# Another instruction order in a fused attention and feed-forward kernel: the last element, the early squares, the folded weights, row 3's routing, maximum 0

## The chip, the cores and the metric

One core of a Trainium2 chip runs the whole kernel. The metric is the device time of one execution in microseconds (us). Three runs of the kernel before gave 920.5 us as their median (919.33 to 921.06).

## The reference, cut to what matters

For each of 16 batch elements (`x` and `ctx` are 128 x 1024, all in float32):

```
def attention(q, k, v, Wq, Wk, Wv, Wo, bo, g):         # q = layernorm(x), k = v = ctx
    qh = softmax(Wq q over each head's 64 rows) / 8     # 8 heads of 64
    kh = softmax(Wk k over the 1024 columns)
    out = Wo (context(kh, Wv v) applied to qh) + bo
    return out / max(norm(out over the 128 rows), 1e-12) * g * sqrt(128)

x = x + tanh(g_xattn) * attention(...)
# feed-forward on y = layernorm(x): 64 experts of rank 16, the top 16 by score
scores = y Wr^T;  gates = softmax(top 16 scores)
h = y A^T (64 x 16 values per row), each expert's 16 times its gate
x = x + tanh(g_ffn) * (h B) * 2
```

## The kernel before, in words

Every product in float32 is made of three passes of 512, 448, 384 or 256 columns on TensorE (helper `three_pass`, lines 59 to 63): a rounded high part and a low part (the remainder) of each operand. ScalarE copies the high part out of PSUM (names `hi_...`) and VectorE subtracts it to give the low part (names `lo_...`).

**Attention stage.** The function `body(b, head, tail, ahead)` is written once for each engine. Body b does the head of element b (queries, keys, their maxima and exponentials, transposes) and the tail of element b-1 (context product, the fold of `Wv` and `Wo` into it, output), and loads the next element. It is laid out for b = 0 and 1, looped for the middle, and laid out for b = 14 (`NB - 2`), 15 (`NB - 1`, called `last` on VectorE) and 16 (tail alone). Each engine runs its instructions in the order in which they are written here; semaphores alone tie the engines together. There is no planner: the order is written by hand.

Steps that matter below, with their lines in the profile:

- queries of block p of 128 columns: TensorE `mm_q` into `psQ`; VectorE `max_q` (L1013); TensorE `shift_q` (L1491) adds the negated maximum; ScalarE `exp_q` (L678, and L685 for block 3); POOL `halve` (L447) and VectorE `sum_q` (L1018, L1021) give the sum; POOL `normalise` (L454); TensorE `tr_q` (L1510) transposes; ScalarE `hi_q` (L693), VectorE `lo_q` (L1027).
- keys of block j: TensorE `mm_k` into `psK`; VectorE `max_k` (L1007); ScalarE `exp_k` (L670); TensorE `tr_k` (L1501); ScalarE `hi_k` (L700), VectorE `lo_k` (L1038).
- context: TensorE `context` (24 passes); ScalarE `hi_kc` (L711), VectorE `lo_kc` (L1043), TensorE `fold` (12 passes of 256 columns), VectorE `scale_m` (L1055), ScalarE `hi_m` (L715), POOL the low part (L546), TensorE `output`, ScalarE `out_o` (L728). Elements 0 to 2 also square their output (L727) and VectorE sums the squares (`part_early`, L969); TensorE's `sum_early` and VectorE's `early_guess` start an inverse square root from them, which POOL finishes.
- in body 0, TensorE multiplies `Wv` and `Wo`; ScalarE (L867) and VectorE (L1304) split the product.
- in body 15, elements 0 and 1 are carried towards the feed-forward part: ScalarE `scale_first` (L742), VectorE `spread` (L1003), POOL `spread_first` and `add_first`, VectorE `stats2_sums` (L1071, L1073) and `std2`, ScalarE `normalise` (L763).

**Feed-forward stage.** Row b of `ffn_body` does for element b: TensorE `up` in three pieces, `sum_u` (L1566) for the norm of element b+2, `down` for element b-1. VectorE routes (`route_step` 0 to 10: copy of scores, top 8, negated maximum, second top 8, gates), multiplies by the gates (L1145), transposes (L1161, L1178). ScalarE exponentiates the scores (`exp_scores`, L811, after step 2), normalises element b+1's input, moves 32 x 256 groups (`move_y`, `move_h`, L778), makes high parts, squares `u` (`square_u`, L750). Row 3 (`third`) runs seven steps of the norm of element 5 before it waits for `h`.

What ScalarE has in row b stands in this order, and the order isn't changed:

```
hi_moved_h(b - 1)
normalise(b + 1, (j + 2) % SLOTS)
exp_scores(b)
move_y(b + 1, j % 2)
hi_moved_y(b + 1)
move_h(b)
square_u(b + 3, ...)
```

## Time and profile before

| | before |
|---|---|
| median of 3 runs | 920.5 us (919.33 to 921.06) |
| the profiled execution, its own time | 921.38 us |
| its span in the trace | 919.5 us |
| mean granted TensorE clock | 0.996 of full |
| TensorE matmul busy | 898.3 us (98%) |
| VectorE busy | 737.2 us (80%) |
| ScalarE busy | 680.6 us (74%) |
| POOL busy | 520.1 us (57%) |

A line of a timeline gives the start in us from the beginning of the span, the duration in us, the engine, the line, the operation, what it writes and reads, and how many instructions of the kind are merged; in brackets at the end stand the time for which the engine was idle before it and what ended that. PE is TensorE, DVE is VectorE, ACT is ScalarE. An operation's duration overlaps the next one's by some 0.07 to 0.1 us on DVE and ACT, and a matmul's (0.39 us for 512 columns) far more, so the distance from start to start is what an instruction costs its engine.

### The profile page before, as it was taken

The numbers are of one execution on the slowest core, as the hardware profiler recorded it, in microseconds if no ns is written. First come the engines' busy times: TensorE is split into PE (matmuls) and PEld (weight loads), VectorE is DVE, ScalarE is ACT, GpSimd is POOL, SyncE is SP. The second block draws the span as 40 slices with busy tenths as digits, with TensorE's granted clock in tenths as the row PEclk, the third lists the DMA queues.
The fourth block names the chain that finished last, engine by engine and source line by source line (L and its number), as shares of the span: only waits on it lengthen the run. The fifth ranks groups of instructions, "written<-read, shape, count | busy, mean of one in ns | idle before, by whom it ended". The sixth has DMA issues, their size and how long they took to land.

```text
span 919.5 us, 15914 instructions
## 1 busy us (share of the span) xinstructions
PE 898.3 (98%) x4732; PEld 760.7 (83%) x4732; DVE 737.2 (80%) x1531; ACT 680.6 (74%) x1392; POOL 520.1 (57%) x342
## 2 busy tenths in 40 slices
PE   7899999999999999999999999999999999999998
PEld 5687887878888888888887799988899989999996
DVE  6888899888888888888887878897877768777642
ACT  4787787687678768777877748678888878888731
POOL 3686777788798789879778958231222212222100
PEclk9999999999999999999999999999999999999999
DMA  4323524443453544344232694112222111212001
GB/s 160 115 82 129 178 78 156 163 144 111 161 185 108 168 139 127 109 135 156 91 115 69 207 354 165 67 68 69 76 71 70 67 64 69 70 67 69 24 24 46
DMA packets 35325, 104.09 MB, mean 113 GB/s; under 512 B 4432, under 2 KB 11600, under 8 KB 35280
## 3 DMA queue, kind: packets, MB, share of 16 engines
q1 hardware_dynamic: 29520, 82.59, 26.2%
q0 software_dynamic: 5472, 20.45, 7.5%
q10 hardware_dynamic: 288, 0.52, 0.1%
q8 instruction: 19, 0.31, 0.1%
q14 instruction: 26, 0.21, 0.1%
HBM read 79.43 MB, written 24.12 MB: 113 GB/s over the span
## 4 chain that ended last, share of the span: by engine, by line
PE 63%; DVE 16%; issue 7%; ACT 7%; POOL 5%; DMA 1%; ACTq 0%; DVEq 0%; POOLq 0%
PE ps L61 19%; PE ps L63 18%; PE ps L62 18%; PE ps L1501 4%; PE ps L1510 3%; DVE qmax L1013 2%; ACT h_raw L778 2%; DVE kmax L1007 2%; PE ps L1491 2%; DVE qT_lo L1027 1%; DVE mt L1055 1%; ACT y_raw L778 1%; ACT qT_hi L693 1%; POOL x L528 1%; POOL qe L454 1%
## 5 line engine op out<-in xcount | busy, mean ns | idle before, releaser
L525 POOL TENSOR_TENSOR rb<-u_in,rb 128x1024 f32<-128x1024 f32 x14 | 33.7, 2410 | 219.0 <-DVE rb L1003 219.0
L454 POOL TENSOR_TENSOR qe<-qe,qrec 128x1024 f32<-128x1024 f32 x64 | 121.2, 1903 | 28.9 <-DVE qrec L1021 28.9
L61 PE MATMUL ps<-aT_hi,yT_hi 128*128 128x448 f32 (+2 forms) x360 | 119.9, 333 | 1.8 <-DVE hg L1145 1.3
L62 PE MATMUL ps<-aT_hi,yT_lo 128*128 128x448 f32 (+2 forms) x360 | 118.7, 330 | 0.0
L63 PE MATMUL ps<-aT_lo,yT_hi 128*128 128x448 f32 (+2 forms) x360 | 118.6, 330 | 0.0
L1027 DVE TENSOR_TENSOR qT_lo<-ps,qT_hi 128x512 fp32r<-128x512 f32 x128 | 82.1, 683 | 42.6 <-ACT qT_hi L693 42.6
L778 ACT ACTIVATE h_raw<-hg 32x256 f32<-32x256 f32 x248 | 103.0, 415 | 17.0 <-DVE hg L1178 14.2
L447 POOL TENSOR_TENSOR qhalf<-qe 128x512 f32<-128x512 f32 x64 | 82.3, 1286 | 32.7 <-ACT qe L685 30.8
L778 ACT ACTIVATE y_raw<-u_in 32x256 f32<-32x256 f32 x216 | 89.5, 414 | 5.8 <-DVE u_in L1161 3.5
L61 PE MATMUL ps<-bT_hi,hT_hi 128*128 128x512 f32 x240 | 93.7, 390 | 0.0
L62 PE MATMUL ps<-bT_hi,hT_lo 128*128 128x512 f32 x240 | 93.5, 390 | 0.0
L63 PE MATMUL ps<-bT_lo,hT_hi 128*128 128x512 f32 x240 | 93.4, 389 | 0.0
L678 ACT ACTIVATE qe<-ps 128x1024 f32<-128x1024 f32 x48 | 49.2, 1025 | 46.4 <-PE ps L1491 46.4
L693 ACT ACTIVATE qT_hi<-ps 128x512 fp32r<-128x512 f32 x128 | 70.7, 598 | 14.9 <-PE ps L1510 13.6
L1007 DVE TENSOR_REDUCE kmax<-ps 128x1 f32<-128x1024 f32 x64 | 77.9, 1216 | 4.0 <-PE ps L63 2.4
L670 ACT ACTIVATE ek<-ps,kmax 128x1024 f32<-128x1024 f32 x64 | 72.3, 1130 | 4.7 <-DVE kmax L1007 3.0
L61 PEld LDWEIGHTS ps<-aT_hi,yT_hi 128*128 128x128 f32 x360 | 68.5, 190 | 5.0 <-issue 1.7
L1510 PE MATMUL ps<-ident,qe 128*128 128x128 f32 x512 | 69.1, 275 | 1.7 <-DVE ekT_lo L1038 1.5
L62 PEld LDWEIGHTS ps<-aT_hi,yT_lo 128*128 128x128 f32 x360 | 68.4, 190 | 2.1
L63 PEld LDWEIGHTS ps<-aT_lo,yT_hi 128*128 128x128 f32 x360 | 68.5, 190 | 1.8
L1510 PEld LDWEIGHTS ps<-ident,qe 128*128 128x128 f32 x512 | 58.0, 140 | 14.0 <-DVE ekT_lo L1038 3.3
L700 ACT ACTIVATE ekT_hi<-ps 128x512 fp32r<-128x512 f32 x100 | 54.5, 601 | 16.0 <-PE ps L1501 16.0
(180 smaller groups left out, 2556.3 us busy)
## 6 DMA issues: line engine op xcount, KB each, us to landing
x_in<-in_x SPq DMA_DIRECT2D x16, 512.0 KB, 4.2
ctx_in<-in_ctx SPq DMA_DIRECT2D x16, 512.0 KB, 4.7
ctxT_in<-in_ctxT SPq DMA_DIRECT2D x16, 512.0 KB, 3.3
ctxT_hi<-in_ctxT POOLq DMA_DIRECT2D x16, 512.0 KB, 3.7
u_scratch<-osb SPq DMA_DIRECT2D x16, 512.0 KB, 2.9
x<-in_x SPq DMA_DIRECT2D x15, 512.0 KB, 4.0
out<-res SPq DMA_DIRECT2D x15, 512.0 KB, 2.9
turn_scratch<-ek SPq DMA_DIRECT2D x14, 512.0 KB, 5.7
```

The lines of the kernel that those rows point to most:

```text
L61: nc.tensor.matmul(psum, whi, mhi, start=start, stop=False)
L62: nc.tensor.matmul(psum, wlo, mhi, start=False, stop=False)
L63: return nc.tensor.matmul(psum, whi, mlo, start=False, stop=stop)
L447: nc.gpsimd.tensor_tensor(qhalf[:, p % 2, :].rearrange("p (h d) -> p h d", d=DH // 2), v[:, :, 0:DH // 2], v[:, :, DH // 2:DH], ALU.add).t ...
L454: nc.gpsimd.tensor_tensor(v, v, w, ALU.mult).then_inc(q_norm, 1)
L670: nc.scalar.activation(to, of, ACT.Exp, bias=kmax[:, j:j + 1], accum_out=ksum[:, j:j + 1]).then_inc(k_exp, 1)
L693: nc.scalar.activation(qT[0][:, :, n * P:n * P + P], psT[:, h, :].rearrange("p (j n) -> p j n", n=P), ACT.Copy).then_inc(q_hi, 1)
L700: nc.scalar.activation(ekT[0][:, 4 * h:4 * h + 4, j * P:j * P + P], psT[:, h, :].rearrange("p (n d) -> p n d", d=P), ACT.Copy).then_inc(k_ ...
L778: last = nc.scalar.activation(dst[32 * q:32 * q + 32, 256 * a:256 * a + 256], src[32 * a:32 * a + 32, 256 * q:256 * q + 256], ACT.Copy)
L1007: nc.vector.tensor_reduce(kmax[:, j:j + 1], psK, axis=AX.XY, op=ALU.max, negate=True).then_inc(k_max, 1)
L1027: nc.vector.tensor_tensor(qT[1][:, :, v], psT[:, h, :].rearrange("p (j n) -> p j n", n=P), qT[0][:, :, v].bitcast(f32), ALU.subtract).then ...
L1510: last = nc.tensor.transpose(psT[:, h, j * P:j * P + P], qe[:, p, w:w + P], ident[:, :])
```

## The change

It moves instructions inside the hand-written order of ScalarE, VectorE and TensorE; none is added, removed or resized, and no semaphore wait is added. On ScalarE: in body 15, the two scalings of elements 0 and 1 come later and the normalisation of element 0 goes from the end of body 15 to behind the last exponentials of queries in body 16; in body 0, the high part of the folded weights comes after three other steps. On VectorE: maximum 0 of the queries precedes the context's low part in every body but the first; the sum of early squares comes some nine steps earlier in bodies 2 to 4; in body 0 the low part of the folded weights comes later; in body 14 the guess for the early norms comes later; in body 15 both spreads come later, and the low part of key block 2 precedes the statistics of element 0 and the sum of query block 1; in row 3 three steps of routing come first and the norm's steps stand together. On TensorE: in body 16 a transpose of queries precedes that of element 0's rows, in body 14 the sum of the early squares follows the context.

```diff
--- before.py
+++ after.py
@@ -813,12 +813,14 @@
             def body(b, head, tail, ahead, early=False):
                 if tail:
                     exp_q(b - 1, 3)
+                if tail and not head:
+                    normalise(0, 0)
                 if head:
                     hi_xn(b, 1)
+                if tail:
+                    hi_kc(b - 1)
                 if head and not ahead:
                     scale_first(0)
-                if tail:
-                    hi_kc(b - 1)
                 if tail and not head:
                     hi_y(0)
                     hi_q(b - 1, 1)
@@ -858,23 +860,23 @@
                     norm_x(b + 1)
                     hi_ctx(b + 1, 0)
                     hi_ctx(b + 1, 1)
+                if head:
+                    hi_k(b, 1)
+                    exp_k(b, 3)
+                if tail:
+                    hi_q(b - 1, 3)
                 if head and not ahead:
                     scale_first(1)
-                if head:
+                if tail and head:
+                    out_o(b - 1, 0, early)
+                if head:
+                    exp_q(b, 2)
                     if not started(b):
                         act.wait_ge(fold_done, 1)
                         for par in range(2):
                             nc.scalar.activation(wvo[0][:, :, par * P:par * P + P],
                                                  psX[:, par, :].rearrange("p (j o) -> p j o", o=P),
                                                  ACT.Copy, scale=DH ** -0.5).then_inc(fold_hi, 1)
-                    hi_k(b, 1)
-                    exp_k(b, 3)
-                if tail:
-                    hi_q(b - 1, 3)
-                    if head:
-                        out_o(b - 1, 0, early)
-                if head:
-                    exp_q(b, 2)
                 if ahead:
                     hi_xn(b + 1, 0)
                 if head:
@@ -889,8 +891,6 @@
                     out_o(b - 1, 1, early)
                 if head:
                     hi_q(b, 0)
-                if head and not ahead:
-                    normalise(0, 0)
 
             exp_k(0, 0)
             body(0, head=True, tail=False, ahead=True)
@@ -1042,6 +1042,16 @@
                 dve.wait_ge(kc_hi, b + 1)
                 nc.vector.tensor_tensor(kc[1][:, :], psX[:, 0, :], kc[0][:, :].bitcast(f32),
                                         ALU.subtract).then_inc(kc_lo, 1)
+
+            def low_fold():
+
+                dve.wait_ge(fold_hi, 2)
+                for par in range(2):
+                    nc.vector.scalar_tensor_tensor(wvo[1][:, :, par * P:par * P + P],
+                                                   psX[:, par, :].rearrange("p (j o) -> p j o", o=P),
+                                                   DH ** -0.5,
+                                                   wvo[0][:, :, par * P:par * P + P].bitcast(f32),
+                                                   ALU.mult, ALU.subtract).then_inc(fold_lo, 1)
 
             def scale_m(b):
 
@@ -1250,24 +1260,24 @@
                     turn_k(b)
                 if ahead and started(b):
                     stats(b + 1)
-                if norms:
-                    early_guess()
                 if ahead and started(b):
                     std(b + 1, range(3))
                 if tail and ahead:
                     sum_q(b - 1, 3)
+                if head and started(b):
+                    max_q(b, 0)
+                if norms:
+                    early_guess()
                 if tail:
                     lo_kc(b - 1)
                 if tail and not head:
                     sum_q(b - 1, 3)
                 if head and started(b):
-                    max_q(b, 0)
                     max_k(b, 1)
+                if early:
+                    part_early(b - 2)
                 if last:
                     sum_q(b - 1, 3)
-                if last:
-                    dve.wait_ge(ctx_lo, 2 * NB)
-                    spread(0, rb_first[0], n_newton, 4 * NEWTON)
                 if tail and not head:
                     lo_y(0)
                     lo_q(b - 1, 1)
@@ -1275,6 +1285,9 @@
                     lo_q(b - 1, 1)
                 if tail:
                     scale_m(b - 1)
+                if last:
+                    dve.wait_ge(ctx_lo, 2 * NB)
+                    spread(0, rb_first[0], n_newton, 4 * NEWTON)
                 if tail and not head:
                     stats2(1, 1)
                     lo_q(b - 1, 2)
@@ -1299,18 +1312,6 @@
                         dve.wait_ge(tanh_done, 1)
                         nc.vector.tensor_scalar(gcol[:, :], g_raw[:, 2:3], gates[:, 0:1], math.sqrt(C),
                                                 ALU.mult, ALU.mult).then_inc(gcol_done, 1)
-                        dve.wait_ge(fold_hi, 2)
-                        for par in range(2):
-                            nc.vector.scalar_tensor_tensor(wvo[1][:, :, par * P:par * P + P],
-                                                           psX[:, par, :].rearrange("p (j o) -> p j o", o=P),
-                                                           DH ** -0.5,
-                                                           wvo[0][:, :, par * P:par * P + P].bitcast(f32),
-                                                           ALU.mult, ALU.subtract).then_inc(fold_lo, 1)
-                if last:
-                    dve.wait_ge(xn_lo, 2 * NB)
-                    spread(1, rb_first[1], n_newton, 4 * NEWTON)
-                if early:
-                    part_early(b - 2)
                 if tail and not head:
                     route(0)
                 if tail:
@@ -1321,13 +1322,20 @@
                 if head:
                     dve.wait_ge(k_exp, 4 * b + 4)
                     nc.vector.reciprocal(krec[:, :], ksum[:, :]).then_inc(k_rec, 1)
+                if last:
+                    dve.wait_ge(xn_lo, 2 * NB)
+                    spread(1, rb_first[1], n_newton, 4 * NEWTON)
                 if ahead:
                     max_k(b + 1, 0)
+                if head and not last:
+                    sum_q(b, 1)
+                if head:
+                    lo_k(b, 2)
+                if not started(b):
+                    low_fold()
                 if last:
                     stats2_sums(0, 0)
-                if head:
                     sum_q(b, 1)
-                    lo_k(b, 2)
                 if last:
                     std2(0, range(4))
                 if head:
@@ -1386,11 +1394,13 @@
                     lo_moved_y(3)
                     spread_u(4)
                 elif third:
-                    norm_steps(5, range(7))
+                    for n in range(3):
+                        route_step(3, n)
                     lo_moved_h(2)
                     turn_y(4, 0)
-                    norm_steps(5, range(7, NRT))
-                    route(3)
+                    norm_steps(5, range(NRT))
+                    for n in range(3, TOP):
+                        route_step(3, n)
                     spread_u(5)
                 else:
                     result(b - 2, (j + 1) % 2, (j + 3) % SLOTS, 2 * i + (j - 1) // 2)
@@ -1627,8 +1637,8 @@
                 if not head:
                     context(b - 1, 0)
                     context(b - 1, 1)
+                    tr_q(b - 1, 1, next(turn))
                     tr_y(0, 0)
-                    tr_q(b - 1, 1, next(turn))
                     fold(b - 1)
                     up(0, 0)
                     tr_q(b - 1, 2, next(turn))
@@ -1640,11 +1650,11 @@
                     up(0, 2)
                     return
 
-                if isinstance(b, int) and b == NB - 2:
-                    sum_early()
                 if tail:
                     context(b - 1, 0)
                     context(b - 1, 1)
+                if isinstance(b, int) and b == NB - 2:
+                    sum_early()
                 if head:
                     if not started(b):
                         pe.wait_ge(wq_low, 1)
```

## Rows read from the trace of the kernel before

**Rows 1.** The page's first part: busy time, share of the span, instructions.

```profile
PE 898.3 (98%) x4732; PEld 760.7 (83%) x4732; DVE 737.2 (80%) x1531; ACT 680.6 (74%) x1392; POOL 520.1 (57%) x342
```

**Rows 2.** Timeline, DVE and then PE, of body 12, one of the loop.

```profile
399.76 0.65 DVE L1043 TENSOR_TENSOR kc_lo<-ps,kc_hi 128x512 fp32r<-128x512 f32 x1
400.45 1.22 DVE L1013 TENSOR_REDUCE qmax<-ps 128x16 fp32r<-128x1024 f32 x1
...
404.06 1.29 DVE L1027 TENSOR_TENSOR qT_lo<-ps,qT_hi 128x512 fp32r<-128x512 f32 x2 [1.03 <-ACT qT_hi L693]
...
401.72 0.70 PE L1491 MATMUL ps<-qmax,ident_r 128*128 128x512 f32 x2
...
403.05 0.36 PE L61 MATMUL ps<-wvo_hi,kc_hi 128*128 128x256 f32 x1
```

**Rows 3.** Timeline, DVE and then PE, of body 3, whose tail is an early element.

```profile
110.67 0.63 DVE L1043 TENSOR_TENSOR kc_lo<-ps,kc_hi 128x512 fp32r<-128x512 f32 x1
111.22 1.21 DVE L1013 TENSOR_REDUCE qmax<-ps 128x16 fp32r<-128x1024 f32 x1
...
114.82 1.29 DVE L1027 TENSOR_TENSOR qT_lo<-ps,qT_hi 128x512 fp32r<-128x512 f32 x2 [1.27 <-ACT qT_hi L693]
...
127.13 1.23 DVE L969 TRANSPOSE_TENSOR_REDUCE part<-osq 128x1024 f32 x1
...
112.48 0.48 PE L1491 MATMUL ps<-qmax,ident_r 128*128 128x512 f32 x1 [0.33 <-DVE qmax L1013]
```

**Rows 4.** Timeline, ACT and then DVE, of body 0.

```profile
27.15 1.06 ACT L867 ACTIVATE wvo_hi<-ps 128x512 fp32r<-128x512 f32 x2
...
30.06 1.28 DVE L1304 SCALAR_TENSOR_TENSOR wvo_lo<-ps,wvo_hi 128x512 fp32r<-128x512 f32 x2
...
36.16 1.21 DVE L1013 TENSOR_REDUCE qtop<-ps 128x16 f32<-128x1024 f32 x1
```

**Rows 5.** Timeline, DVE, ACT and then PE, of body 15, the last with a head.

```profile
499.87 1.19 DVE L1003 STREAM_TRANSPOSE rb_first<-nr 128x1024 f32<-128x1024 f32 x1
...
516.58 1.25 DVE L1071 BATCH_NORM_STATS2 bn<-x 128x6 f32<-128x512 f32 x2
...
518.94 1.22 DVE L1038 TENSOR_TENSOR ekT_lo<-ps,ekT_hi 128x512 fp32r<-128x512 f32 x2
...
521.84 1.28 DVE L1038 TENSOR_TENSOR ekT_lo<-ps,ekT_hi 128x512 fp32r<-128x512 f32 x2
...
511.30 1.15 ACT L742 ACTIVATE u_first<-u_first,gcol 128x1024 f32<-128x1024 f32 x1 [1.48 <-DMA u_first<-u_scratch]
...
517.25 1.09 ACT L700 ACTIVATE ekT_hi<-ps 128x512 fp32r<-128x512 f32 x2
...
505.61 0.50 PE L61 MATMUL ps<-qT_hi,mt_hi 128*128 128x512 f32 x1 [1.21 <-POOL mt_lo L546]
...
522.66 1.16 PE L1510 MATMUL ps<-ident,qe 128*128 128x128 f32 x8 [0.38 <-DVE ekT_lo L1038]
```

**Rows 6.** Timeline of the feed-forward rows 2 to 5: DVE, ACT and then PE.

```profile
611.96 1.24 DVE L1161 STREAM_TRANSPOSE u_in<-u_in 128x1024 f32<-128x1024 f32 x1
...
614.68 0.35 ACT L811 ACTIVATE ex<-sc,neg_top 128x64 f32<-128x64 f32 x1 [2.83 <-DVE neg_top L1104]
614.94 6.81 ACT L778 ACTIVATE y_raw<-u_in 32x256 f32<-32x256 f32 x16
...
600.76 0.44 PE L61 MATMUL ps<-aT_hi,yT_hi 128*128 128x448 f32 x1 [1.33 <-DVE hg L1145]
...
624.54 0.47 PE L61 MATMUL ps<-aT_hi,yT_hi 128*128 128x448 f32 x1 [0.41 <-DVE yT_lo L1173]
...
654.85 0.40 PE L1566 MATMUL ps<-part,sel 128*128 128x32 f32 x2 [2.14 <-DVE part L1209]
```

**Rows 7.** Busy time by stretch: after the stretch, its length, PE, PEld, DVE, ACT, POOL busy (instructions), granted clock, DMA share, GB/s.

```profile
31.00:34.00 3.00, 3.00 (x11) 2.45 (x10) 1.42 (x3) 0.87 (x3) 2.83 (x2) 0.50 0.09 29
...
655.00:659.00 4.00, 4.00 (x16) 4.00 (x17) 3.34 (x11) 1.92 (x5) 0.00 (x0) 0.57 0.62 217
```

## The prediction

> **What bounds the kernel now.** I read the page first, then the timeline engine by engine at each moved instruction, then the granted clock of the stretches around TensorE's long waits. TensorE is busy for 98% of the span [rows 1], and its passes follow each other at a fixed distance through nearly all of it. So a moved instruction matters only where TensorE stands still, or where the move makes it stand still. Four places have such stalls near the edits: bodies 2 to 4, where the shift of query block 0 waits for its maximum (0.33 us in body 3) [rows 3]; body 15 (1.21 us for the low part of the scaled context, 0.38 us for a low key part) [rows 5]; the feed-forward rows 2 to 5 (1.33, 0.41 and 2.14 us) [rows 6]; and body 0. Two of them drag a second cost behind them: TensorE worked at a granted clock of 0.50 in 31 to 34 us and 0.57 in 655 to 659 us [rows 7], its 1.2 GHz level for most of that time, which costs 3 x 0.50 = 1.5 us and 4 x 0.43 = 1.7 us.
>
> **Maximum 0 ahead of the context's low part, in the loop.** The maximum starts at 400.45, right behind the low part of 399.76, and looks delayed by it. It isn't: its six passes ended at about 400.41, as the low part did. With the new order VectorE waits for TensorE and starts at the same 400.45. The low part then ends at about 400.45 + 1.15 + 0.65 = 402.25, later by 1.85 us; behind it stand the key maximum (0.45 us later) and the low query part, which has 1.03 us of idle time before it that absorbs this. Who waits for the low part is the fold, at 403.05: 0.8 us of slack is left. The transpose and the shift at 401.72 see no difference [rows 2]. I take 0 for each of the twelve undisturbed bodies. Bounds: gain of 0.03 each (the distance of the two starts), loss of 0.1 each should the slack be smaller than it looks.
>
> **Bodies 2 to 4.** Here VectorE is late. The low part begins at 110.67, the maximum at 111.22, though its input was there at 110.80, so the new order starts it at 110.84: 0.38 us earlier, and 0.55 in body 2. But the sum of early squares, 1.23 us, now stands between key maximum 1 and the low query part at 114.82, in an idle time of 1.27 us [rows 3]. Step by step for body 3: maximum 110.84, context's low part 111.98, key maximum 112.53, sum of squares 113.65, low query part 114.81. That is where it begins today. Behind it stand the scaling by the sums, its high and low parts, and the output, which TensorE waits for. So the stall moves from the shift to the output. I take -0.2 for body 2, 0 for 3 and 4. Bounds: -1.3 (all three gains kept), +0.5 (the sum costs more than the gain). Taking the sum away from its old place at 127.13 gains nothing, since VectorE waits there for ScalarE a few steps on.
>
> **Body 0.** The high part of the folded weights (1.06 us) leaves the path to the exponentials of key block 3, which hold TensorE until 30.33; but the transpose ends only at 27.5, so about 0.6 is gained there, and POOL's second low part of the next context, ending at 31.0, holds the rest. The low part of the folded weights (1.28 us) leaves a place where VectorE was idle anyway and lands right before query maximum 3 at 36.16 [rows 4], on the path to the transpose that starts the context product. Gain of 1.0 upstream against 1.2: +0.2. Bounds: -0.9 (the half clock of 31 to 34 us disappears too) and +0.8.
>
> **Body 14.** Two small VectorE steps and one small matmul change place within slack; the fold waits for the first of them, which is done 1 us before it. 0, bounds -0.2 and +0.3.
>
> **Body 15, first half.** The spread (1.19 us) stood before the low query part and delayed the chain to the output at 505.61. Moved behind the scaling, it frees 1.1 us, of which the order of the maximum takes back 0.35: -0.77 there. The spread now delays query maximum 1 and key maximum 2 by 0.3, so at the transpose of query block 3 about 0.5 is left.
>
> **Body 15, second half.** ScalarE's second scaling (1.15 us at 511.30) moves behind the high part of query block 3, right ahead of the output's copy, exponentials 2 and the high part of key block 2. That one, at 517.25 today, comes at 517.55: 0.5 to 0.8 gained ahead, 1.06 lost. VectorE's low part of key block 2 can start 0.62 later, at 518.17. Behind it now stand the element's statistics and the sum of query block 1, which today run from 516.58 to 518.94 (2.36 us), while VectorE idles before 518.17. Low key part 3, today 2.90 us behind low part 2, starts at 518.17 + 2.36 + 2.90 = 523.43, not 521.84; the transpose of query block 0, 0.82 behind that, at 524.25, not 522.66 [rows 5]. The whole body is 1.6 us longer, and TensorE is idle for 2.9 us in one piece. POOL's normalisation of query block 1 waits for that sum; behind it are queued its DMA issues for the `A` weights and two additions, all about 1.3 us later, with the users later by as much. SP's loads wait for the end of the context and shift with it.
>
> **The clock there.** An idle time of 2.14 us was followed by the low level, one of 1.33 us was not [rows 6, 7]. After 2.9 us I expect a stretch at 1.2 GHz, part of which falls into the idle time: half to all of 1.7 us, I take +1.0. Bounds 0 and 1.9.
>
> **Body 16.** Element 0's normalisation leaves the place ahead of exponentials 3 and comes right behind them; those follow the late transpose, so they end when they do today. Two transposes change places. The rows of element 0 are ready when TensorE gets there: 0, bounds -0.2 and +0.5, since VectorE's low part of them is within 0.2 us of the path.
>
> **Row 3.** ScalarE waits for 2.83 us for the negated maximum, and behind that wait stands the moving of element 4's groups at 614.94, whose input is ready at 613.2 [rows 6]. With the three steps of routing first, the groups move 1.7 us earlier. The norm steps that VectorE did in idle time now come behind: gates and transpose are 0.6 later, so ScalarE's second move starts 1.3 earlier. The stall at 624.54 (0.41) goes; the one at 654.85 ends the same chain (moves, squares, sum of squares), so it ends 1.3 earlier, and since TensorE is 0.4 ahead by then, 1.3 us is the net gain and the stall shrinks from 2.14 to about 1.2. That is below the 1.33 that left the clock alone, so I take the 1.7 us of slow clock back as well, rounded up to 1.8 with the slow restart: -3.1. Bounds: -0.4 and -3.8.
>
> **Sum.** +0.2 - 0.2 + 1.6 + 1.0 - 3.1 = -0.5 us. The profiled execution took 921.4 us, the median of the runs 0.9 less, 920.5; the difference is applied to the median: 920.0 us. About 0.2% (1.8 us) is what a measurement of this kernel can tell from no change.
>
> **A rule on the clock.** The Trainium skill, TensorE: Matmul & The Clock Gate, Part 1, says that half clock is the default state which activity lifts, and that the monitor runs free of the kernel's start, so that its switches fall differently from run to run. The trace agrees that long idle times come before the low level; one trace can't show the scatter. By that rule both clock terms would be even chances, +0.5 and -0.9, and the sum would be +0.3.
>
> **Rivals.**
> - *All four gains hold* (chance 0.28). The early bodies keep their 1.3 us, and TensorE keeps its clock after the gap of body 15. For it: the sum of squares fits into 1.27 us of idle time to within 0.04 [rows 3], and an overlap of 0.1 decides. Against it: the working above uses those overlaps already. 0.2 - 1.3 + 1.6 - 3.1 = -2.6: 917.9 us.
> - *The clock decides against the change* (0.15, slower). The place is body 15's gap before the context. It costs the full 1.7 behind 1.6, and the shorter gap in row 5 still ends in the low level, so only 1.3 is gained there. It decides if the low level can follow a gap as short as 1.2 us; body 0 speaks for it, where it came after a wait shorter than 1.5. 0.2 - 0.2 + 3.3 - 1.3 = +2.0: 922.5.
> - *The loop pays* (0.08, slower). If the fold's slack of 0.8 is gone, for example because the low part waits longer behind the maximum, each of 13 bodies loses 0.2: -0.5 + 2.6 = +2.1: 922.6.
> - *Row 3's stall isn't set by ScalarE's moves* (0.05, slower). Then the reorder doesn't do what it says, POOL's residual sets the time, and only 0.4 is gained: +2.2: 922.7.
> - The forecast holds the remaining 0.44, with a range of its own of 918.6 to 921.6; 0.06 of it lies more than 0.2% below.
>
> So faster by over 0.2%: 0.28 + 0.06 = 0.34; slower: 0.28; within: 0.38. The range of 917.0 to 923.2 takes in the first rival's bound and all the slower ones, each with half a microsecond more.
>
> **What would show it.** Right: the shift of query block 0 in the loop keeps its distance of 1.27 us from the start of its maximum; in body 3 the stall before it goes and the one before the output grows; the output in body 15 starts about 0.8 earlier, but the transpose before the context about 1.6 later, behind low key part 3; ScalarE's wait for the negated maximum in row 3 nearly goes, and the sum in row 5 waits about 1.2 us, with a clock of 1.00 behind it. Wrong: a fold that waits for the context's low part; a gap before the context below 1 us; a clock near 0.5 still standing behind row 5's sum.

## The result, and the profile after

The changed kernel takes 923.35 us (median of 5 runs, 922.31 to 925.61), the kernel before 920.5 us in the runs beside it (919.33 to 921.75). The ratio is 1.0033 with a 95% interval of 1.0018 to 1.0049: slower by 2.9 us, where 0.5 us faster was forecast, and just above the range.

The profiled execution took 922.31 us, 0.9 more than that of before: it was the fastest of its five, while that of before was above its median. So the traces explain 0.9 of the 2.9 us directly. The trace of before holds two stretches at the low clock level and that of after one, so the two aren't equal in this; the part on the clock comes back to it.

The page's first part, of after. Busy times are those of [rows 1] to within 1.8 us, in a span 1.0 us longer: no work was added, so the change is all in waits.

```profile
span 920.5 us, 15914 instructions
PE 897.1 (97%) x4732; PEld 758.9 (82%) x4732; DVE 738.2 (80%) x1531; ACT 680.4 (74%) x1392; POOL 520.5 (57%) x342
```

Both traces are cut at the same TensorE instructions. Each row is the distance of two starts, in us of the profiled executions:

| stretch | before | after | difference | forecast |
|---|---|---|---|---|
| start to the first context pass (body 0) | 39.03 | 39.27 | +0.24 | +0.2 |
| its context pass in body 2 to that in body 5 | 97.96 | 97.39 | -0.57 | -0.2 |
| fold of body 5 to fold of body 13 (loop) | 256.53 | 256.43 | -0.10 | 0 |
| fold of body 13 to fold of body 14 | 32.25 | 33.39 | +1.14 | 0 |
| fold of body 14 to row 0's up part | 65.42 | 68.46 | +3.04 | +2.6 |
| row 0's up part to row 5's sum | 122.11 | 120.87 | -1.24 | -1.3 |
| row 5's sum to row 6's | 24.69 | 23.13 | -1.56 | -1.8 |

They add up to +0.95, the difference of the spans to 0.01, and row 6's sum to the last one is 161.85 us in both. One row is far from the forecast by its path: body 14. This is its timeline, of after, DVE, POOL and then PE.

```profile
464.04 1.23 DVE L1013 TENSOR_REDUCE qmax<-ps 128x16 fp32r<-128x1024 f32 x1 [0.67 <-PE ps L63]
465.18 0.25 DVE L995 TENSOR_SCALAR ns<-ps 128x96 f32<-128x96 f32 x1
465.46 1.90 DVE L67 TENSOR_SCALAR nr<-ns 128x96 int32<-128x96 int32 x1
467.28 0.68 DVE L1043 TENSOR_TENSOR kc_lo<-ps,kc_hi 128x512 fp32r<-128x512 f32 x1
...
463.54 3.76 POOL L454 TENSOR_TENSOR qe<-qe,qrec 128x1024 f32<-128x1024 f32 x2
...
468.02 0.39 PE L61 MATMUL ps<-wvo_hi,kc_hi 128*128 128x256 f32 x1 [1.12 <-DVE kc_lo L1043]
```

The root step of the early norms, line 67 on 128 x 96 numbers, takes 1.90 us. In the trace of before the same instruction, ahead of the context's low part, took 0.21 us:

```profile
462.44 0.20 DVE L995 TENSOR_SCALAR ns<-ps 128x96 f32<-128x96 f32 x1
462.67 0.21 DVE L67 TENSOR_SCALAR nr<-ns 128x96 int32<-128x96 int32 x1
463.99 0.68 DVE L1043 TENSOR_TENSOR kc_lo<-ps,kc_hi 128x512 fp32r<-128x512 f32 x1
...
464.02 3.77 POOL L454 TENSOR_TENSOR qe<-qe,qrec 128x1024 f32<-128x1024 f32 x2
```

In the old place POOL's halving ended 0.14 us after the root began (461.52 + 1.29 = 462.81). In the new order it comes while POOL multiplies the query block by its reciprocal sums (two instructions of 1.9 us). It ends at 465.46 + 1.90 = 467.36, about when the second of these does (463.54 + 3.76 = 467.30). The context's low part stands behind it, and the fold, which has 0.8 us of slack in the loop by the prediction's working, waits: 1.12 us by the row, 1.37 us counted from where its next pass could have started.

The trace of before holds the same sight already, in row 1 of the feed-forward part: a small step of the routing, SBUF to SBUF, takes 1.83 us and ends at 572.21, with POOL's fourth instruction of a row (561.66 + 10.49 = 572.15). In the 15 other feed-forward rows it takes 0.25 or 0.26 us.

```profile
570.38 1.83 DVE L1130 TENSOR_SCALAR gate<-gsel,grec 128x64 f32<-128x64 f32 x1
...
561.66 10.49 POOL L484 TENSOR_TENSOR bT_lo<-b_raw,bT_hi 128x1024 fp32r<-128x1024 f32 x4
```

Body 15, of after, DVE, ACT and then PE:

```profile
516.62 1.21 DVE L1003 STREAM_TRANSPOSE rb_first<-nr 128x1024 f32<-128x1024 f32 x1
518.88 1.29 DVE L1038 TENSOR_TENSOR ekT_lo<-ps,ekT_hi 128x512 fp32r<-128x512 f32 x2 [1.05 <-ACT ekT_hi L700]
520.09 1.28 DVE L1081 BATCH_NORM_STATS2 bn<-x 128x6 f32<-128x512 f32 x2
521.64 0.63 DVE L1018 TENSOR_REDUCE qsum<-qhalf 128x16 f32<-128x512 f32 x1
523.06 1.21 DVE L1013 TENSOR_REDUCE qtop<-ps 128x16 f32<-128x1024 f32 x1
524.19 1.28 DVE L1038 TENSOR_TENSOR ekT_lo<-ps,ekT_hi 128x512 fp32r<-128x512 f32 x2
...
515.73 1.14 ACT L742 ACTIVATE u_first<-u_first,gcol 128x1024 f32<-128x1024 f32 x1
518.25 1.09 ACT L700 ACTIVATE ekT_hi<-ps 128x512 fp32r<-128x512 f32 x2
...
505.47 0.50 PE L61 MATMUL ps<-qT_hi,mt_hi 128*128 128x512 f32 x1 [0.44 <-POOL mt_lo L546]
525.02 1.94 PE L1520 MATMUL ps<-ident,qe 128*128 128x128 f32 x8 [2.65 <-DVE ekT_lo L1038]
```

The output's wait fell from 1.21 to 0.44 us [rows 5], and the transpose of query block 0 waits 2.65 us for the last low key part, with TensorE idle for 2.81 us in one piece (2.9 was forecast). Low key part 2 could start at 518.88, and low key part 3 starts 5.31 us behind it, where it was 2.90 [rows 5].

Body 0, of after: VectorE's low part of the folded weights stands right ahead of query maximum 3, as forecast. What wasn't forecast is in the last row:

```profile
30.54 1.10 ACT L877 ACTIVATE wvo_hi<-ps 128x512 fp32r<-128x512 f32 x2
35.20 1.28 DVE L1050 SCALAR_TENSOR_TENSOR wvo_lo<-ps,wvo_hi 128x512 fp32r<-128x512 f32 x2
36.39 1.22 DVE L1013 TENSOR_REDUCE qtop<-ps 128x16 f32<-128x1024 f32 x1
37.52 1.28 DVE L1038 TENSOR_TENSOR ekT_lo<-ps,ekT_hi 128x512 fp32r<-128x512 f32 x2
...
31.04 0.50 PE L61 MATMUL ps<-ctx_hi,wk_hi 128*128 128x512 f32 x1 [0.20 <-POOL ctx_lo L413]
38.35 1.16 PE L1520 MATMUL ps<-ident,qe 128*128 128x128 f32 x8 [2.36 <-DVE ekT_lo L1038]
```

The wait before the transpose that opens the context product was [1.16] in the trace of before (1.53 us of idle time), and is 2.36 (2.72 us idle). Ahead of it nearly nothing was gained, since the keys of block 1 now wait for POOL's low part (31.04).

The loop and the feed-forward rows went as forecast. Body 12 (maximum, context's low part, shift) and row 5's sum, of after:

```profile
399.98 1.22 DVE L1013 TENSOR_REDUCE qmax<-ps 128x16 fp32r<-128x1024 f32 x1 [0.63 <-PE ps L63]
401.12 0.68 DVE L1043 TENSOR_TENSOR kc_lo<-ps,kc_hi 128x512 fp32r<-128x512 f32 x1
...
401.26 0.70 PE L1501 MATMUL ps<-qmax,ident_r 128*128 128x512 f32 x2
402.59 0.36 PE L61 MATMUL ps<-wvo_hi,kc_hi 128*128 128x256 f32 x1
...
604.53 0.44 PE L61 MATMUL ps<-aT_hi,yT_hi 128*128 128x448 f32 x1 [1.35 <-DVE hg L1155]
627.75 0.36 PE L61 MATMUL ps<-aT_hi,yT_hi 128*128 128x448 f32 x1
657.35 0.40 PE L1576 MATMUL ps<-part,sel 128*128 128x32 f32 x2 [1.51 <-DVE part L1219]
```

The shift follows the start of its maximum by 1.28 us, as by 1.27 before [rows 2]. Row 3's stall of 0.41 is gone, and row 5's has fallen from 2.14 to 1.51 [rows 6]. By stretch, of after (columns as in [rows 7]):

```profile
31.00:34.00 3.00, 2.96 (x17) 2.44 (x17) 1.93 (x3) 2.69 (x6) 3.00 (x2) 1.00 0.05 12
38.00:44.00 6.00, 5.64 (x29) 4.76 (x30) 5.12 (x9) 4.92 (x19) 1.33 (x2) 1.00 0.14 57
525.00:528.00 3.00, 2.98 (x11) 2.75 (x12) 2.75 (x9) 1.60 (x5) 3.00 (x6) 0.50 0.93 267
657.00:660.00 3.00, 2.65 (x16) 2.66 (x17) 2.82 (x5) 1.13 (x1) 0.00 (x0) 1.00 0.96 339
```

The low level stands behind body 15's stall alone; in the trace of before it stood in body 0 and behind row 5's stall.

### The profile page after: what moved, and what is told of

It is laid out like the page before. It is cut to its first block, busy times and chain, and to the rows that moved or that the text cites. A ratio compares the mean times of both kernels' runs of the same rounds, so it can differ in the third digit from the quotient of the medians.

```text
span 920.5 us, 15914 instructions
## 1 busy us (share of the span) xinstructions
PE 897.1 (97%) x4732; PEld 758.9 (82%) x4732; DVE 738.2 (80%) x1531; ACT 680.4 (74%) x1392; POOL 520.5 (57%) x342
## 4 chain that ended last, share of the span: by engine, by line
PE 71%; DVE 16%; ACT 5%; issue 5%; POOL 2%; DMA 0%; DVEq 0%; ACTq 0%; POOLq 0%
PE ps L61 21%; PE ps L63 20%; PE ps L62 20%; PE ps L1520 5%; PE ps L1511 4%; ACT h_raw L778 3%; DVE kmax L1007 2%; DVE qmax L1013 2%; PE ps L1501 1%; DVE mt L1065 1%; DVE qT_lo L1027 1%; POOL x L528 1%; DVE ekT_lo L1038 1%; DVE hg L1188 1%; POOL rb L525 1%
## 5 line engine op out<-in xcount | busy, mean ns | idle before, releaser
L1013 DVE TENSOR_REDUCE qmax<-ps 128x16 fp32r<-128x1024 f32 x48 | 58.6, 1221 | 14.0 <-PE ps L63 13.2
```

Source lines behind the costliest of these rows:

```text
L1013: nc.vector.tensor_reduce(top[:, p % 2, :], psQ.rearrange("p a (h d) -> p (a h) d", d=DH), axis=AX.X, op=ALU.max, negate=True).then_inc(q_ ...
```

## The experiments

In the diffs, lines with + are the experiment's. Times are medians with the lowest and highest run; kernels of one batch share the runs of before. The stretches of all kernels, in us of the profiled executions:

```
                      ctx 1   bodies  loop    fold 13  fold 14  row 3 up  sum 5   idle    idle
                      to 2    2 to 5  5-13    to 14    to up 0  to sum 5  to 6    body 0  body 15
before                31.80   97.96   256.53  32.25    65.42    54.09     24.69   1.53    0.54
after                 31.79   97.39   256.43  33.39    68.46    52.82     23.13   2.72    2.81
body 14 back          33.36   97.39   256.45  32.21    67.19    52.82     23.15   2.73    2.84
root reads PSUM       33.05   97.44   256.50  32.01    67.20    52.82     23.15   2.73    2.82
row 3 alone           31.80   97.90   256.49  32.24    65.30    52.82     23.15   1.53    0.50
body 15 back          33.31   97.37   256.47  33.38    65.92    52.82     23.15   2.73    0.56
statistics back       33.18   97.39   256.44  33.39    65.90    52.85     24.69   2.73    0.56
body 0 back           31.84   97.41   256.41  33.39    68.71    52.83     24.70   1.53    2.80
squares back          33.90   96.50   256.43  33.40    67.14    52.82     24.71   2.73    2.82
first try             31.80   96.56   256.43  32.23    67.24    52.83     24.69   1.53    -
row 3 and maximum 0   31.79   96.54   256.55  32.18    65.58    52.81     23.15   1.53    0.49
with the late spread  31.83   96.50   256.54  32.20    65.24    52.81     23.14   1.53    0.54
three places back     31.82   97.40   256.42  32.20    65.97    52.81     23.15   1.54    0.56
```

"ctx 1 to 2" is from the first context pass to the next, "bodies 2 to 5" from context pass to context pass, "up 0" row 0's up part, "sum 5 to 6" from row 5's sum to row 6's, "idle" TensorE's idle time before the first query transpose of a context product, counted from where its next pass could have started, which is 0.15 to 0.38 us more than the wait in brackets. Two columns show the clock: "ctx 1 to 2" is 31.8 where the granted clock stays at 1.00, and 33.05 to 33.90 where a low stretch lies in it; "sum 5 to 6" is 23.15 or 24.7 in the same way, so that stretch costs 1.55 us.

**Body 14 undone.** VectorE's root step goes back ahead of the context's low part, and TensorE's summing pass ahead of the context passes; all else is the changed kernel.

```
+                if norms:
+                    early_guess()
                 if ahead and started(b):
                     std(b + 1, range(3))
...
-                if norms:
-                    early_guess()
                 if tail:
                     lo_kc(b - 1)
```

> The changed kernel with body 14 as it was before: the guess of the early norms ahead of the context's low part and of query maximum 0, and TensorE's small sum ahead of the context. Theory (the guess's second step, held for 1.90 us behind POOL's normalisation, delays the context's low part and so the fold): the wait of 1.37 us before the fold at 468.0 us goes, the distance between the first fold passes of bodies 14 and 15 drops from 31.7 us of the changed kernel by some 1.4, and the median by 1.3 to 1.6 us, to about 921.9. Rival (body 14 only looks longer, since body 15 takes back what it loses): the wait goes but the fold of body 15 comes no earlier, and the time stays at 923.3.

Measured: 922.20 us (921.32 to 923.43), ratio 1.0016 [1.0008, 1.0025], beside 920.95 for before. The interval overlaps that of the changed kernel, so here and in the next runs the place is shown by the trace, and the median agrees with it. The two folds are 32.21 us apart again, 1.18 less than in the changed kernel, and the root takes 0.21 us:

```profile
463.72 0.21 DVE L67 TENSOR_SCALAR nr<-ns 128x96 int32<-128x96 int32 x1
466.84 0.68 DVE L1043 TENSOR_TENSOR kc_lo<-ps,kc_hi 128x512 fp32r<-128x512 f32 x1
...
468.31 0.36 PE L61 MATMUL ps<-wvo_hi,kc_hi 128*128 128x256 f32 x1
```

So 1.2 us of the loss is made in body 14. Here body 15's stall of 2.84 us had no low level behind it, while a stretch in body 1 did, where the changed kernel's trace has 1.00:

```profile
38.00:41.00 3.00, 2.76 (x13) 2.30 (x14) 2.16 (x5) 2.08 (x8) 1.12 (x1) 0.70 0.29 119
41.00:44.00 3.00, 3.00 (x11) 2.45 (x10) 2.95 (x5) 2.91 (x13) 0.54 (x1) 0.73 0.09 38
525.00:528.00 3.00, 2.60 (x15) 2.23 (x16) 2.82 (x10) 1.94 (x7) 3.00 (x6) 1.00 0.93 271
```

**The root reads PSUM.** Order and wait stay as in the changed kernel; only the source of the root step is the sums in PSUM and not their copy in SBUF. That leaves out the lower bound on the sums for the root.

```
-                first_root(r, s).then_inc(n_guess, 1)
+                first_root(r, psN_early.rearrange("p (e n) -> p e n", e=EARLY)).then_inc(n_guess, 1)
```

> The changed kernel, with the order as it is, but the guess's second step (the first root) reads the sums in PSUM rather than their copy in SBUF; it leaves out the floor under the sum for this first guess, which no value reaches. Theory (the step of 1.90 us has one input and one output in SBUF and waits for the port that POOL's running multiplication holds): with its input in PSUM it takes about 0.2 us as at its old place, the context's low part starts 1.7 us earlier, and the fold waits 0 to 0.2 us. First rival (the step is held by its semaphore or by the queue): it still takes 1.9 us and the fold still waits 1.3. Second rival (the place itself is too late, whatever the step takes): the fold still waits by 1 us or more.

Measured: 922.85 us (921.19 to 923.92), ratio 1.0022 [1.0012, 1.0032], which doesn't tell it from the changed kernel. Timeline of body 14, DVE and POOL, of this kernel:

```profile
467.96 0.25 DVE L995 TENSOR_SCALAR ns<-ps 128x96 f32<-128x96 f32 x1
468.25 0.26 DVE L67 TENSOR_SCALAR nr<-ps 128x96 int32<-128x96 int32 x1
468.42 0.68 DVE L1043 TENSOR_TENSOR kc_lo<-ps,kc_hi 128x512 fp32r<-128x512 f32 x1
...
466.33 3.77 POOL L454 TENSOR_TENSOR qe<-qe,qrec 128x1024 f32<-128x1024 f32 x2
468.20 1.91 POOL L454 TENSOR_TENSOR qe<-qe,qrec 128x1024 f32<-128x1024 f32 x1
```

The last row is the second of the two multiplications by itself. The root starts 0.05 us behind it, where in the changed kernel it came 0.06 us behind (465.46 and 465.40), and takes 0.26 us instead of 1.90. The folds are 32.01 us apart, and the fold doesn't wait. So the root isn't late because of its place in the order alone, nor because its inputs are late: it is held when it reads SBUF and not when it reads PSUM. The Trainium skill states this in SBUF — State Buffer, section "SBUF: two separate sides": VectorE's second port pair is shared with GpSimd, and whichever starts first has it for its whole instruction. VectorE: DVE Perf Modes, "What auto-detection actually checks", says which 32-bit operations take both ports: a single source, with it and the destination in SBUF and the outermost size even, or equal in both. The traces agree, with 1.90 us against 0.26. In the changed kernel the step ahead of it (line 995, source in PSUM, same shape) took 0.25 us beside the same multiplication. SBUF on both sides isn't enough to be held: in the changed kernel a step on 128 x 1 numbers at 462.35 (line 80) took 0.14 us and the reciprocal of 128 x 16 at 463.12 took 0.25 us, both beside POOL's instruction of 462.29 to 463.58.

**Row 3 alone.** The kernel before, with row 3's new order and nothing else.

```
-                    norm_steps(5, range(7))
+                    for n in range(3):
+                        route_step(3, n)
                     lo_moved_h(2)
                     turn_y(4, 0)
-                    norm_steps(5, range(7, NRT))
-                    route(3)
+                    norm_steps(5, range(NRT))
+                    for n in range(3, TOP):
+                        route_step(3, n)
```

> The kernel before with the new order of row 3 alone. Theory (ScalarE's wait of 2.83 us for the negated maximum goes, its moves run 1.3 to 1.7 us earlier, the stall before the sum in row 5 shrinks and the half clock behind it goes): the distance from the first up-projection pass of row 3 (600.76) to the sum in row 5 (654.85) falls from 54.1 to 52.8 us, 1.3 less, the clock behind it is 1.00, and the median is 2 to 3 us below 920.5. Rival (the gain in the changed kernel came from the clock by chance, not from the order): the distance is the same within 0.3 us or the half clock stands behind a shorter stall, and the time is 919 to 920.5.

Measured: 917.71 us (917.36 to 920.1), ratio 0.9974 [0.9963, 0.9984]. Row 3's up part to row 5's sum is 52.82 us instead of 54.09, and the clock behind the sum stays up:

```profile
652.59 0.40 PE L1568 MATMUL ps<-part,sel 128*128 128x32 f32 x2 [1.52 <-DVE part L1209]
...
656.00:660.00 4.00, 4.00 (x33) 4.00 (x32) 3.29 (x18) 3.88 (x11) 0.00 (x0) 1.00 0.00 0
```

The path gives 1.3 us, as forecast, and the medians differ by 3.2: most of the rest fits what the low level behind row 5's sum costs (24.69 - 23.15 = 1.54 us). The mean granted clock of the timed runs says the same: where it is 1.000, seven runs of this kernel take 917.4 to 917.8 us and nine of before 918.9 to 920.2 (median 919.1), 1.7 apart; and it is 1.000 in 7 runs of 12 here, but in 9 of the 79 of before in all batches. That the low level went because the stall got shorter is not shown by this alone.

**Body 15, two ways.** First VectorE's order of the last statistics and ScalarE's second scaling are put back; then VectorE's order alone:

```
-                if head and not last:
-                    sum_q(b, 1)
+                if last:
+                    stats2_sums(0, 0)
                 if head:
+                    sum_q(b, 1)
                     lo_k(b, 2)
                 if not started(b):
                     low_fold()
-                if last:
-                    stats2_sums(0, 0)
-                    sum_q(b, 1)
```

> The changed kernel with two moves of body 15 undone: VectorE takes the statistics of element 0 and the sum of query block 1 ahead of low key part 2 again, and ScalarE's second scaling stands ahead of the high key part 1 again. The first spread behind the scaling stays. Theory (the second half of body 15 is a chain on VectorE, and the two moves put 1.1 us of idle time into it while the work behind it stays): TensorE's gap before the transpose of query block 0 falls from 2.81 us to below 1, that transpose starts 1.7 to 2.3 us earlier against the start of body 15, the clock in the context stays at 1.00, which gives another 1.4; together 3 us off the median, to about 920.3. Rival (the gap comes from the late stall of body 14 or from exponentials 2, not from the order of these two): the gap stays over 2 us and the time within 0.5 of 923.3.

> The changed kernel with only the VectorE half of body 15's second part undone (statistics of element 0 and sum 1 ahead of low key part 2); ScalarE's second scaling stays late. Theory (two parts, 1.1 us of idle time ahead of low key part 2 and the scaling's 1.06 us on ScalarE): the idle time is filled, so the gap before the transpose of query block 0 falls from 2.8 to about 1.1 us, with up to 1 us of new stall before key transpose 3 as in the kernel with both undone, and body 15 plus 16 comes out 1.5 to 2.5 us shorter than in the changed kernel. Rival (the late scaling alone is the cause): the sum of the stalls before key transpose 3 and query transpose 0 stays at 2.8.

Measured: 921.74 us (920.4 to 924.55), ratio 1.0013 [1.0003, 1.0022], with both back, and 921.91 us (920.05 to 923.25), ratio 1.0014 [1.0004, 1.0023], with VectorE's alone. The stall of 2.81 us becomes two shorter ones. TensorE in the kernel with VectorE's order back:

```profile
522.57 1.16 PE L1509 MATMUL ps<-ident,ek 128*128 128x128 f32 x8 [0.80 <-DVE ekT_lo L1038]
525.51 1.16 PE L1518 MATMUL ps<-ident,qe 128*128 128x128 f32 x8 [0.41 <-DVE ekT_lo L1038]
```

The stretch from fold 14 to row 0 is 65.92 and 65.90 us, against 68.46, or 67.2 where no low level follows. So VectorE's order costs 1.3 us of path, and ScalarE's late scaling nothing that can be seen. The median expected with both back, 920.3, was missed by 1.4 us: the clock in body 15 stays up, but a low stretch in body 1 is left. About 0.5 us over the kernel before (65.42) is left too: low key part 2 is late for the transpose of key block 3 (0.80 us). The second spread stands ahead of the statistics now, which may be why; it wasn't tried.

**Body 0 undone.** Both edits of body 0 (ScalarE's and VectorE's folded weights) go back.

```
+                    if not started(b):
+                        act.wait_ge(fold_done, 1)
...
                     hi_k(b, 1)
                     exp_k(b, 3)
...
-                if not started(b):
-                    low_fold()
```

> The changed kernel with the folded weights where they were, on ScalarE ahead of high key part 1 and on VectorE behind low key part 1; all else as changed. Theory (the low part of the weights, 1.3 us on VectorE ahead of query maximum 3, opens a gap of 2.7 us before the transpose that starts the context, while the move on ScalarE brings nothing, since POOL's low part of the next context is ready only at 30.95 us): the first context pass comes at 38.1 to 38.3 us where the clock stays up and at 39.0 where it falls at 31 us, the gap before the transpose is 1.5 us instead of 2.7, the half clock at 40 to 43 us is gone, and the median drops by 1 to 2 us, to 921.5 to 922. Rival (body 0 costs nothing, as forecast: +0.2): the context starts within 0.3 us of 39.27 and the time stays at 923.3.

Measured: 921.92 us (920.61 to 924.46), ratio 1.0019 [1.0008, 1.0029], beside 920.87 for before.

```profile
37.67 1.16 PE L1519 MATMUL ps<-ident,qe 128*128 128x128 f32 x8 [1.16 <-DVE ekT_lo L1038]
...
38.00:44.00 6.00, 6.00 (x31) 4.93 (x30) 4.89 (x10) 4.93 (x19) 2.90 (x3) 1.00 0.40 161
```

The idle time is 1.53 us again, and from the first shift (28.96, 28.42 in the changed kernel) to the context pass it is 9.63 us against 10.85, both at a full clock. The two edits weren't undone one by one; the rows put the 1.2 us down to VectorE's, since the low part of the folded weights (1.28 us) stands right ahead of query maximum 3 and the wait behind it grew by 1.20. The stretch in body 1 has a clock of 1.00 here, as in all profiles with the short stall, and the changed kernel was the only one of six with the long stall that had it. Here there are low levels in body 15 and behind row 5's sum.

**The early squares back.** The changed kernel with the sum of squares where it was.

```
-                if early:
-                    part_early(b - 2)
                 if last:
                     sum_q(b - 1, 3)
...
+                if early:
+                    part_early(b - 2)
                 if tail and not head:
                     route(0)
```

> The changed kernel with the sum of the early squares back behind low key part 1 in bodies 2 to 4; maximum 0 stays ahead of the context's low part. Theory (the sum holds up the low query part and with it the low part of the scaled context, which the output waits for): the waits before the shift and the output in these bodies go from 0.24 and 0.29 to 0.1 and 0.2, and bodies 2 to 4 take 32.1 us each instead of 32.4, together 0.9 to 1.2 us less from body 2's first context pass to body 5's. Rival (the early bodies are longer because of ScalarE's squares, wherever VectorE sums them): the distance stays within 0.2 us.

Measured: 924.44 us (922.2 to 925.4, 6 runs), ratio 1.0042 [1.0027, 1.0056]. The stretch of the early bodies is 96.50 us, 0.9 less than in the changed kernel. The median doesn't show it: the interval overlaps that of the changed kernel, and the profiled execution has a clock of 0.50 from 38 to 44 us and 0.71 from 660 to 664. The traces of all kernels agree with the 0.9: 96.50 to 96.56 us in the four that have the maximum early and the squares in their old place, 97.37 to 97.44 in the seven that have both moved.

**A first try at a better version.** From the changed kernel: body 0, body 14 and the squares back, ScalarE's second scaling later still, and the statistics and query sum 1 behind low key part 3. The diff shows only the last of these.

```
                 if head:
                     max_q(b, 3)
                     lo_k(b, 3)
+                if last:
+                    sum_q(b, 1)
+                    stats2_sums(0, 0)
+                    std2(0, range(4))
```

> A version meant to beat both: row 3's new order; maximum 0 ahead of the context's low part; both spreads of body 15 late; ScalarE's second scaling behind high key part 2, where it waits anyway; statistics of element 0, the sum of query block 1 and the rest of the inverse root behind low key part 3 on VectorE; element 0's normalisation late; body 0, body 14 and the sum of early squares as before. From the parts: row 3 -3.2, early bodies -1.1, body 15 -0.8 at the first output and -1.0 to -1.5 at the second half. Expected: 914.5 to 915.5 us, TensorE's gap before query transpose 0 below 0.3 us. If the row 5 stall of 1.7 us grows by what TensorE gains earlier, less: 916.5.

Measured: 919.31 us (917.87 to 922.39), ratio 0.9992 [0.998, 1.0003], 4 to 5 us above what was expected and not to be told from the kernel before. From fold 14 to the context passes it is 55.12 us (520.43 - 465.31), 1.0 less than with row 3 alone, and the stall before query block 0 is gone. But row 0's up part comes 67.24 behind the fold, 1.9 later than with row 3 alone: it waits for the low part of element 0's rows. Their normalisation needs the statistics, and query sum 1 and POOL's multiplication are later too; which of these sets it wasn't separated.

```profile
532.55 0.47 PE L61 MATMUL ps<-aT_hi,yT_hi 128*128 128x448 f32 x1 [2.46 <-DVE yT_lo L1166]
```

**Row 3 and maximum 0.** Now built up from the kernel before: row 3's order, and the maximum ahead of the context's low part in every body, with the squares in their old place.

```
                 if tail and ahead:
                     sum_q(b - 1, 3)
+                if head and started(b):
+                    max_q(b, 0)
                 if tail:
                     lo_kc(b - 1)
...
                 if head and started(b):
-                    max_q(b, 0)
                     max_k(b, 1)
```

> The kernel before with two parts of the change: row 3's order and maximum 0 ahead of the context's low part (the early squares stay in their old place). If the gains of the parts add: the stretch of bodies 2 to 5 from one context pass to the next is 96.6 us as in the kernel with the squares in their old place (97.9 with row 3 alone), the FFN as with row 3 alone (52.8 us from row 3's up part to row 5's sum), so 1.3 us less than row 3 alone: 916.2 to 916.8 us, ratio to before about 0.9955. Rival: time saved by the early bodies is waited for later, at body 14's fold (POOL's part is ahead of TensorE there), and the ratio stays 0.997.

Measured: 916.33 us (916.25 to 917.99, 5 runs), ratio 0.9956 [0.9943, 0.997], beside 920.97 for before. Bodies 2 to 5 take 96.54 us, 1.36 less than with row 3 alone, and of this at most 0.3 is waited for later (fold 14 to row 0: 65.58 against 65.30). Where the mean clock is 1.000, four runs take 916.25 to 916.66 us, below all seven with row 3 alone. So the maximum's move gains 1.4 us, of which the moved squares give back 0.9 in the changed kernel (96.50 against 97.39 by the run above).

**The same with the late spread.** In the last body the first spread goes behind the scaling, and ScalarE's high context part ahead of its first scaling.

```
-                if last:
-                    dve.wait_ge(ctx_lo, 2 * NB)
-                    spread(0, rb_first[0], n_newton, 4 * NEWTON)
...
                 if tail:
                     scale_m(b - 1)
+                if last:
+                    dve.wait_ge(ctx_lo, 2 * NB)
+                    spread(0, rb_first[0], n_newton, 4 * NEWTON)
```

> The kernel of the two parts, with the late spread(0) in the last body and ScalarE's high part of the folded key context ahead of scale_first(0); the statistics stay where they were. If the first half of body 15 is a gain by itself: the gap before its output passes is 0.4 to 0.7 us instead of 1.2 and the stretch from body 14's fold to row 0's up part falls from 65.4 to 64.9 us, ratio 0.0005 under the kernel of two parts. Rival: the late spread pushes VectorE's later work (scale of the maps, low key parts) by its 1.2 us, and a wait of the same size stands before key transpose 3 or the first query transpose (65.9 us).

Measured: 916.25 us (915.89 to 916.77, 5 runs), ratio 0.9951 [0.9938, 0.9965]. Fold 14 to row 0 is 65.24 us, 0.34 less than without it, where 0.5 was expected: the wait before the output fell from 1.57 to 0.44 us, but most of that is waited for later in the body. The two intervals overlap, so the step is shown by the traces alone; the version is 4.5 us faster than the kernel before.

**Three places back.** The changed kernel with body 0's two edits, body 14 and VectorE's order in body 15 undone together, by the diffs above.

> The changed kernel with its three named places undone: body 0's two edits, body 14's root step and summing pass, and VectorE's order of the last body's statistics; all else is kept. If these three places hold the whole loss: no wait before body 14's fold, 1.5 us or less before the first query transpose of body 0, no wait of 2.8 us in body 15 but 0.95 and 0.56; by the single runs undone (1.0, 1.4 and 1.4 us under the changed kernel) the sum is 3.8 us, so 919.3 us or less, ratio 0.998 to 0.999. Rival: the single gains overlap (the half clock that one stall brings is brought by another), and the ratio stays at 1.001 or above.

Measured: 918.39 us (917.29 to 920.2, 11 runs), ratio 0.9977 [0.9968, 0.9986], 0.0056 under the changed kernel (5.2 us). One by one the three gave 0.0014 (body 0), 0.0017 (body 14) and 0.0019 (VectorE's order), together 0.0050. So they hold the whole loss and 2 us more, and they nearly add: 0.0006 is less than these intervals can tell.

## Why the prediction was wrong

**The step that failed is body 14**: "two small VectorE steps and one small matmul change place within slack ... 0, bounds -0.2 and +0.3". By the durations of before (0.20 and 0.21 us for the two steps) the slack was there. But in its new place the root took 1.90 us. POOL's multiplication from 464.02 to 467.79, in the trace of before, lies over the new place, and doesn't appear in this step of the working; nor does the routing step of 1.83 us that the same trace shows beside POOL. The step is worth 1.14 us by the trace, and 0.0017 of the time by undoing it.

**Body 0 was mis-sized.** Its term of +0.2 was 1.2 of cost against 1.0 of gain. Both edits undone give 1.2 net (10.85 - 9.63 us), the size of the cost alone. The gain isn't there: with the first shift at 28.42 in both, the transpose of key block 3 starts at 34.84 in the changed kernel and at 34.86 in that with row 3 alone, at a full clock. The row of after names POOL's low part of the next context as what the keys of block 1 wait for. That +0.24 was measured is chance: the trace of before had lost its time there to a half clock, the trace of after had not. Against the kernel with row 3 alone, at a full clock (first context pass at 38.10), body 0 is 1.17 slower.

**The clock.** The term for body 15 was right where the low level came: 68.46 us with it, 67.2 without, so 1.3 us against the +1.0 taken; it came in two of five profiles with that stall. But a stall of 2.7 us in body 0 wasn't forecast, and five of the six profiles that have it show a low level behind it, at a cost of 1.3 to 2.1 us (33.05 to 33.90 against 31.8). The sixth is that of the changed kernel itself.

The mean clock of the timed runs shows how much of the 2.9 us is clock. In the profiles it falls by about 0.002 with each low stretch: 1.000 with row 3 alone (none), 0.998 in after (one), 0.996 in before (two). At 0.996 the changed kernel has three runs of 923.2 to 924.3 us, before 39 of 920.6 to 922.0 (median 921.3). At 0.998 the changed kernel has its profiled run of 922.31, before 18 of 919.9 to 921.4 (median 920.4). So at the same clock the change costs some 2 us. The rows of the traces give the same where they are taken at a full clock: +1.2 (body 0), -0.6 (early bodies), -0.1, +1.1 (body 14), +1.8 (body 15) and -1.2 (row 3) are +2.2, where the forecast, without its clock terms, had +0.3. The rest of the 2.9 us, some 0.9, fits one low stretch more in the changed kernel's median run (0.996) than in that of before, whose 920.5 us lies below all 39 runs at 0.996. The forecast had -0.8 for the clock. In which stretch the timed runs lose it isn't on record; body 0's stall is the most probable place, and that stays argued.

The last sum in "A rule on the clock" is wrong in itself: with +0.5 for body 15 and -0.9 for row 5 it is 0.2 - 0.2 + 1.6 + 0.5 - 1.3 - 0.9 = -0.1, not +0.3.

**What was right.** Row 3: -2.8 against -3.1, its stall and the slow clock behind row 5's sum gone; alone it is worth 0.0026. The loop: -0.1 against 0. The early bodies: the move of the squares gives back most of what the maximum gains (0.9 of 1.4; -0.57 measured, -0.2 forecast). Body 15's path: 67.2 - 65.4 = +1.8 against +1.6, with an idle time of 2.81 against 2.9, by the order that the text gives.

The three slower rivals lie at 922.5 to 922.7, near the measured 923.35, and none is right in its cause. The loop doesn't pay (-0.10), and row 3's reorder does what it says. That the clock decides against the change (922.5) is half right: the low level can stand behind body 15's stall, but it went behind row 5's, and bodies 14 and 0 are not in it. So their nearness is luck. With +1.1 for body 14 and +1.0 for body 0 the forecast's own sum would have been -0.5 + 2.1 = +1.6, or 922.1, and with another low level behind body 0's stall 923.7.

## What to carry to other kernels

Before a VectorE step with SBUF on both sides is moved, look at what POOL does in the new place: a step of 0.2 us can take as long as POOL's instruction has left (1.90 us here), though not every such step is held (a 128 x 1 step wasn't), and all that is queued behind it moves too. Compare a forecast with a profile whose clock is known in every stretch, and count each new TensorE stall as a possible half clock in addition (here 0.9 to 2.1 us). Parts of a reorder are best tried from the kernel before, one at a time: here two of the edits are worth 4.1 us by themselves (0.0044), and the rest of the change takes that away and 3 us more.

## What the runs showed of the hardware that was not expected

The root step: 0.21 us where no multiplication of POOL runs, 1.90 us beside POOL's multiplication from SBUF to SBUF, 0.26 us beside the same multiplication once its source is PSUM. A hold shows as a long duration of the VectorE step, not as idle time before it.

The low clock level after a stall differs between executions. Behind idle times of 2.7 us in body 0 it was there in five profiles of six; behind 2.8 us in body 15 in two of five; behind 1.53 us in body 0 in none of seven. Ahead of that transpose, from 31 to 34 us, the clock was 0.50 in before and in "three places back", after waits of at most 1.5 us, and 1.00 in the others that have the same order there. Behind row 5's sum it was there in five profiles, after waits of 1.63 us (four) and 2.14 us, and not in the eight others, after waits of 1.51 to 1.62 us. The two groups are 0.01 us apart, so this sets no limit. The Trainium skill, TensorE: Matmul & The Clock Gate, Part 1, says that the monitor runs free of the kernel's start; the profiles of body 0 and body 15 agree. The clock's terms should have been chances from the start, one for each stall.
